# Two fused layers on one core: where the first layer's per-batch mixing stands, before or after the large product

## The reference

```python
att   = softmax(mlp(cond))                          # 32 batches x 8 experts
agg_w = einsum('bk,koi->boi', att, weight)          # a 128x128 matrix of each batch
agg_b = att @ bias_k                                # 128 values of each batch
u     = einsum('boi,bih->boh', agg_w, x) + agg_b[:, :, None]
W_eff = W + sum_e coeffs*scales * Bf_e @ A_e        # 2048x2048, one for all batches
x1    = x + einsum('bsd,od->bso', u, W_eff) + bias
```

## Time and profile before

| | |
|---|---|
| median of 3 runs | 2640.07 us (2638.24 to 2641.44) |
| profiled execution, its own time | 2640.44 us |
| its span, first to last instruction | 2638.5 us |
| PE busy | 2570.8 us, 97% of the span |
| DVE busy | 1837.5 us, 70% |
| ACT busy | 1001.5 us, 38% |
| POOL busy | 955.3 us, 36% |
| DMA | 541.04 MB, mean 205 GB/s |

### The profile page before, as it was taken

The page is one execution under the profiler, slowest core; times in us unless marked ns, Lnnn a source line. Parts: engine busy times, 40 slices in busy tenths (PEclk is TensorE's granted clock), DMA queues, the critical chain, the costliest instruction groups (busy, mean ns, idle before and its releaser), DMA issues. The chain is left out here.

```text
span 2638.5 us, 39106 instructions
## 1 busy us (share of the span) xinstructions
PE 2570.8 (97%) x12090; PEld 2111.6 (80%) x12090; DVE 1837.5 (70%) x2671; ACT 1001.5 (38%) x1631; POOL 955.3 (36%) x826
## 2 busy tenths in 40 slices
PE   7899999999999999999999999999999999999997
PEld 6678888888888888888888778888888888888775
DVE  6555555865555855567444668888888888888776
ACT  3211211322122322233222455555555555555563
POOL 2265654556553554332232312222222222222231
PEclk9999999999999999999999999999999999999998
DMA  8845554755544776576455664576767676767687
GB/s 306 310 168 184 195 174 152 266 170 200 190 156 169 244 226 215 172 239 208 156 167 182 196 178 130 158 219 205 230 206 222 210 223 203 231 212 223 192 272 246
DMA packets 417283, 541.04 MB, mean 205 GB/s; under 512 B 36248, under 2 KB 270064, under 8 KB 417072
## 3 DMA queue, kind: packets, MB, share of 16 engines
q1 hardware_dynamic: 315584, 307.40, 38.9%
q10 hardware_dynamic: 77376, 154.27, 15.6%
q0 software_dynamic: 24112, 76.80, 9.3%
HBM read 309.72 MB, written 228.61 MB: 204 GB/s over the span
## 5 line engine op out<-in xcount | busy, mean ns | idle before, releaser
L427 PE MATMUL ps_c<-w_hi,ring_hi 128*128 128x512 f32 x1792 | 714.1, 398 | 9.6 <-DVE ring_lo L910 5.2
L427 PE MATMUL ps_c<-w_hi,ring_lo 128*128 128x512 f32 x1792 | 708.6, 395 | 0.0
L427 PE MATMUL ps_c<-w_lo,ring_hi 128*128 128x512 f32 x1792 | 708.3, 395 | 0.0
L574 ACT ACTIVATE ring_hi<-raw_n 128x512 fp32r<-128x512 f32 x384 | 241.2, 631 | 901.6 <-DVE raw_n L871 247.3
L1290 POOL DMA_INDIRECT y_d<-y_s,idx x128 | 147.2, 1150 | 736.3 <-ACT y_s L1458 688.0
L427 PEld LDWEIGHTS ps_c<-w_hi,ring_hi 128*128 128x128 f32 x1792 | 338.7, 189 | 87.1 <-DVE ring_lo L910 10.2
L1425 ACT ACTIVATE kern<-ps_up 128x512 f32<-128x512 f32 x512 | 306.2, 598 | 260.3 <-PE ps_up L1308 235.4
L427 PEld LDWEIGHTS ps_c<-w_hi,ring_lo 128*128 128x128 f32 x1792 | 338.4, 189 | 79.2
L427 PEld LDWEIGHTS ps_c<-w_lo,ring_hi 128*128 128x128 f32 x1792 | 338.8, 189 | 76.4
L1542 DVE TENSOR_TENSOR g_lo<-kern,g_hi 128x512 fp32r<-128x512 f32 x512 | 354.7, 693 | 41.0 <-ACT g_hi L1429 20.6
L931 DVE TENSOR_TENSOR r_early<-ps_c,r_early 128x512 f32<-128x512 f32 x256 | 176.8, 691 | 284.3 <-PE ps_c L427 284.3
(11 more groups left out here) (199 smaller groups left out, 3843.5 us busy)
## 6 DMA issues: line engine op xcount, KB each, us to landing
u_d<-raw_n ACTq DMA_DIRECT2D x64, 512.0 KB, 3.3
x_d<-r_early ACTq DMA_DIRECT2D x128, 256.0 KB, 3.4
x_d<-x_s ACTq DMA_DIRECT2D x128, 256.0 KB, 2.6
raw_n<-u_d SPq DMA_DIRECT2D x64, 512.0 KB, 3.7
u_s<-x_d SPq DMA_DIRECT2D x496, 64.0 KB, 2.7
z_d<-x_s SPq DMA_DIRECT2D x120, 256.0 KB
rear<-y_d SPq DMA_DIRECT2D x112, 256.0 KB
rear<-x_d SPq DMA_DIRECT2D x112, 256.0 KB
```

Of the source, the lines that this page charges most:

```text
L427: mm = nc.tensor.matmul(bank, a[:, dc, :], w[k][:, dc, :], start=(first and dc == 0 and n == 0), stop=(dc == 3 and n == 2), skip_group_che ...
L574: nc.scalar.activation(ring_hi[g % RING][:].rearrange("p a n -> p (a n)"), ring_raw[p][k], ACT.Copy).then_inc(hi_ready, 1)
```

## The change

W_eff is applied to x itself, and each batch's mixed matrix afterwards, to the finished pieces.
- SP loads x turned (`x_t`, a further input laid out on the host) straight into `raw`; `make_u`, `take_u`, the store of u and its DRAM array are gone.
- In sweeps 1 and 2 (quads 0 to 15) a piece is only copied out of PSUM and stored (half sums, in `x1_d`). Beside that x + bias is made by POOL in pieces of their own (`res`, a ring of 4; `add_bias`) and stored to a DRAM array `xb_d`.
- In sweeps 3 and 4 (from quad `FINAL` = 16) each of the 8 finished pieces of a quad is split (`split_v` on ACT and DVE), multiplied by its batch's matrix (`mix_v` on PE: 3 matmuls of 512 columns, in slots 6, 7, 12, 13 of the quad and 0 to 3 of the next), and added to x + bias + agg_b times row sum (`take_mixed` on DVE; `add_bias_of_mix` on ACT and `add_e` on POOL make and add the last term). The matrices of a quad are split too (`split_agg`).
- The row sums of W_eff are gathered by POOL and DVE in `sums`, and added over the partitions by two float32 matmuls in slot 5 of quads 16 and 24 (`sum_rows`).
- The ring of split operands has 4 buffers in place of 6, and the operands are made 3 items ahead in place of 4. `EARLY` is 16, so 16 chunks are split in the second layer's steps. The table of rooms is another.
- In the opening the mixed matrices are made in slots 2 and 7 of quad 0, and PE's first products wait for the weights one at a time.

```diff
@@ -38,14 +38,19 @@
 
 
 QUADS = 32
-EARLY = 24
+FINAL = QUADS // 2
+EARLY = 16
 ITEMS = 14
-RING = 6
+RING = 4
 LAST = QUADS * ITEMS
+TRAIL = 8
 HALVES = ((0, 0), (1, 1), (0, 1), (1, 0))
 TILES = 32
 R11, R12, R21, R22 = range(4)
 T_B11, T_B21, T_T2, T_T1, T_T3, T_T4, T_B22 = range(7)
+PIECES = ((R11, 0), (R11, 1), (R22, 0), (R22, 1), (R21, 0), (R21, 1), (R12, 0), (R12, 1))
+MIX_SLOT = (6, 7, 12, 13, 14, 15, 16, 17)
+BIAS_SLOT = (5, 6, 8, 9, 10, 11, 13, 14)
...
         def freed_chunks(q, t):
 
-            n = 2 * (ITEMS * (q - QUADS + 1) + t - 2)
+            n = 2 * (ITEMS * (q - QUADS + 1) + t - 6)
             return range(n, n + 2) if 0 <= n < EARLY else ()
...
-            def load_x(q, j):
-                b = batch(q, j)
-                wait(sp, u_mm, turn(q - 1, j) + 1 if q else 0)
-                if q:
-                    sp.wait_ge(r_set, residuals(q - 1, j // 2, (R12, R21)[j % 2]))
-                sp.dma_start(x_s[j], x[b, :, half_cols(q)]).then_inc(x_or_u_in[j], 16)
...
+            def load_raw(q, j):
+
+                if q == 0:
+                    room_free(sp, (8, 4, 9, 5)[j])
+                else:
+                    sp.wait_ge(lo_ready, ITEMS * (q - 1) + (11 if j % 2 else 13) + j // 2)
+                sp.dma_start(raw[j], x_t[HALVES[sweep(q)][1], batch(q, j), :, :]).then_inc(raw_in[j], 16)
...
+            def load_res(n):
+
+                m = n % 4
+                if n < 4:
+                    room_free(sp, (7, 7, 3, 3)[m])
+                    if m >= 2:
+                        sp.wait_ge(aggw_mm, 8)
+                wait(sp, sh.res_out[m], 16 * (n // 4))
+                sp.dma_start(res[m], piece(x.rearrange("b c (s q) -> b c s q", s=S) if n < 8 * FINAL else xb_d, n)).then_inc(res_in[m], 16)
...
-                if t == 25:
-                    room_free(sp, 6)
-                    load_x(0, 0)
-                    room_free(sp, 7)
-                    load_x(0, 2)
-                if t == 28:
-                    sp.wait_ge(aggb_out, 16)
-                    sp.wait_ge(aggw_out, 16 * 8)
-                    load_agg(0, 0)
-                    load_agg(0, 2)
-                if t == 30:
-                    load_bias(0)
-            for j in (1, 3):
-                room_free(sp, (2, 3)[j // 2])
-                load_x(0, j)
-                load_agg(0, j)
-
...
+                if t in (22, 24, 26, 28):
+                    load_raw(0, {22: 0, 24: 2, 26: 1, 28: 3}[t])
+            room_free(sp, 3)
+            sp.dma_start(experts, cond_w).then_inc(experts_in, 16)
+            room_free(sp, 2)
+            load_bias(0)
...
-            for p in range(2):
-                sp.wait_ge(sh.r_out[p][R11], 16 * QUADS)
-                sp.wait_ge(sh.r_out[p][R22], 16 * QUADS)
+            for m in range(4):
+                sp.wait_ge(sh.res_out[m], 16 * 2 * QUADS)
...
-            def make_u(q, j):
-                n = turn(q, j)
-                pe.wait_ge(x_or_u_in[j], 16 * (q + 1))
-                pe.wait_ge(agg_in[j], 32 * (q + 1))
-                wait(pe, u_ready, n - 1)
-                for dc in range(8):
-                    mm = nc.tensor.matmul(ps_v[:, n % 2, dc * P:(dc + 1) * P], x_s[j][:, dc * P:(dc + 1) * P],
-                                          agg[:, j, :], start=True, stop=True)
-                mm.then_inc(u_mm, 1)
...
+            def mix_v(n):
+
+                i = n - 8 * FINAL
+                blk, p = PIECES[n % 8]
+                j = 2 * p + blk // 2
+                pe.wait_ge(vlo_ready, i + 1)
+                wait(pe, mixed, i - 3)
+                if n % 8 == 0:
+                    pe.wait_ge(agglo_ready, n // 8 - FINAL + 1)
+                if n % 64 == 0:
+                    pe.wait_ge(rs_ready, n // 64 - 1)
+                if n == 8 * 26 + 3:
+                    pe.wait_ge(ctx_read, 1)
+                for a, v in ((agg_hi, v_hi), (agg_hi, v_lo), (agg_lo, v_hi)):
+                    mm = nc.tensor.matmul(ps_w[n % 4], a[:, j, :], v[n % 2][:], start=(a is agg_hi and v is v_hi),
+                                          stop=(a is agg_lo))
+                mm.then_inc(mix_mm, 1)
...
+            def sum_rows(half):
+
+                pe.wait_ge(sums_ready, sums_count(23 if half else 15))
+                pe.wait_ge(aggw_ready, 8)
+                wait(pe, mixed, 64 * half)
+                for n in range(2):
+                    mm = nc.tensor.matmul(ps_w[n], ones[:].to_broadcast([P, P]), sums[half][:, n * 512:(n + 1) * 512],
+                                          start=True, stop=True)
+                mm.then_inc(rs_mm, 1)
...
+            def split_v(n):
+                i = n - 8 * FINAL
+                blk, p = PIECES[n % 8]
+                v_ready(act, n)
+                wait(act, mix_mm, i - 1)
+                nc.scalar.activation(v_hi[n % 2][:], r_s[p][blk], ACT.Copy).then_inc(vhi_ready, 1)
...
+            def add_bias_of_mix(n):
+
+                b, half, sub = place_of(n)
+                act.wait_ge(rs_ready, half + 1)
+                act.wait_ge(res_set, n - 1)
...
+                if n == 8 * 24:
+                    act.wait_ge(mix_out, 16 * 24)
+                nc.scalar.activation(e_room(n), rs_s[:, sub * 512:(sub + 1) * 512], ACT.Identity,
+                                     scale=aggb_s[:, b:b + 1]).then_inc(e_ready, 1)
...
+            def store_res(n):
+                if n < 8 * FINAL:
+                    act.wait_ge(res_set, n + 1)
                 else:
...
+                    act.wait_ge(mixed, n - 8 * FINAL + 1)
+                act.dma_start(piece(xb_d if n < 8 * FINAL else x1_d, n), res[n % 4]).then_inc(sh.res_out[n % 4], 16)
...
-                if ITEMS * q + t + 4 < LAST:
-                    split(ITEMS * q + t + 4)
+                ahead = product_from(q, t, 3)
+                if ahead and ahead != (0, 0):
+                    split(*ahead)
...
+            def add_bias(n):
+                sub = place_of(n)[2]
+                pool.wait_ge(res_in[n % 4], 16 * (n // 4 + 1))
+                pool.wait_ge(bias_in, 16 * (sweep(n // 8) + 1))
+                nc.gpsimd.tensor_tensor(res[n % 4], res[n % 4], bias_s[:, sub * 512:(sub + 1) * 512], ALU.add).then_inc(res_set, 1)
...
-            def take_u(q, j):
-                n = turn(q, j)
-                dve.wait_ge(u_mm, n + 1)
-                dve.wait_ge(agg_in[j], 32 * (q + 1))
-                if q == 0:
-                    room_free(dve, (8, 4, 9, 5)[j])
-                else:
-                    dve.wait_ge(lo_ready, ITEMS * (q - 1) + (11 if j % 2 else 13) + j // 2)
-                    dve.wait_ge(u_out[j], 16 * q)
-                nc.vector.tensor_tensor(raw[j].rearrange("p (c o) -> p c o", o=P),
-                                        ps_v[:, n % 2, :].rearrange("p (c o) -> p c o", o=P),
-                                        bc[:, j, :].unsqueeze(1).to_broadcast([P, 8, P]), ALU.add).then_inc(u_ready, 1)
...
+            def split_v(n):
+                i = n - 8 * FINAL
+                blk, p = PIECES[n % 8]
+                dve.wait_ge(vhi_ready, i + 1)
+                wait(dve, mix_mm, i - 1)
+                nc.vector.tensor_tensor(v_lo[n % 2][:], r_s[p][blk], fp32(v_hi[n % 2][:]), ALU.subtract).then_inc(vlo_ready, 1)
+
+            def take_mixed(n):
+                i = n - 8 * FINAL
+                dve.wait_ge(mix_mm, i + 1)
+                dve.wait_ge(res_set, n + 1)
+                nc.vector.tensor_tensor(res[n % 4], ps_w[n % 4], res[n % 4], ALU.add).then_inc(mixed, 1)
```

More of the change, by code:

```diff
@@ L789, in slot @@
[L789 to L794 removed]
+                    if t in (10, 11):
+                        sum1(q + 1, t - 10)
+                    if t in (12, 13):
+                        sum3(q + 1, t - 12)
+                    if t == 13:
+                        sum2(q + 1, 0)
@@ L795, in slot @@
                         load_early(n)
-                if q == QUADS - 1 and t == 2:
-                    for n in range(4, EARLY):
-                        load_early(n)
-            quads(slot, -7)
+            quads(slot, -4)
         @block.vector
```

590 lines of the change are left out of this document (310 added, 280 removed).

## The result

The changed kernel takes 2761.9 us (2759.96 to 2764.51), against 2640.7 for the kernel before in the same comparison: a ratio of 1.0461, 95% interval 1.0443 to 1.0479. It is 4.6% slower; 2644 was forecast, with a range of 2619 to 2664. The profiled execution has a span of 2758.1 us, 119.6 more than before.

What follows compares the result with a forecast made beforehand. PE, busy for 97% of the span, was taken as the bound. Its work summed to -33.9 us; waits at weight changes and quad 26, seam and second layer made it +3.8: 2644 us, 0.15% more, range 2619 to 2664.

Steps and rivals of the forecast that it cites:

- opening: Tile loads before the first product: SP's stall goes, room waits give back some 2.2 us; -8.5 us, bounds -11 and -3.
- quad 0: First quad: four u's and most of two PE waits go, 42.4 us for 59.9, -17.5.
- quads 1 to 14, first weight change: Without u's 39.07 us a quad, -100.8; PE waiting for DVE's low parts at the first weight change, +3.
- quads 15 to 31, without the last five pieces: Piece matmuls (+89.3 for all 128), row sums +3.6, second and third weight changes +3 and +15, quad 26 +2; +109.4 together.
- seam, with these pieces: Between the layers: a longer chain from last product to barrier, +12.2 us, ends 6 and 16, beside five pieces' matmuls, 3.5.
- second layer: Its start: eight more weight chunks are four more steps, half a microsecond or so each; +2.5 us, ends 0 and 6.
- Rivals 1 and 2: First: stalls are light, 2624 us, chance 0.32. Second: opening gains all, seam costs only 6 for 12.2, 2635, chance 0.06.
- Rival 4: Early quads: transfers land late, each of 8 quads waits 1 us; 2652 us, chance 0.07.
- Rival 3: Late quads: DVE's order binds, one late link is a PE wait, 1 us a quad in 16; 2660 us, chance 0.14.
- Rival 5: Late quads: DVE and POOL instructions run one after the other, 4.1 us a quad; 2698 us, chance 0.05.
- Weight changes: PE waits for late DVE: +3 us at each of the first two, +15 at the third (13 waiting, 2 lower clock).
- In quad 26: Slot 5: context matmuls wait for the last piece of quad 25, three DVE instructions ahead; +2 us.

Runs made afterwards that it cites:

- the relaxed order: Changed kernel with every weight-piece step placed behind the one it waits for, and ACT's store of x + bias one slot later: 2699.6 us, ratio 1.0236.

## Why the prediction was wrong

By its own terms, in span (quad starts of both traces):

| term | forecast | measured |
|---|---|---|
| opening | -8.5 | -9.3 (first product at 116.34 for 125.61) |
| quad 0 | -17.5 | -18.2 |
| quads 1 to 14, first weight change | -97.8 | -30.7 (617.1 for 647.8) |
| quads 15 to 31, without the last five pieces | +109.4 | +153.2 (817.4 for 664.2) |
| seam, with these pieces | +15.7 | +18.3 |
| second layer | +2.5 | +6.3 |

**The step that failed** is "Quads 1 to 14 without u's: 14 x 39.07 = 547.0", with its sentence that they keep their cover. I priced what PE does in such a quad and took from the quads with u's that nothing else is late there. The change had moved the weight pieces to earlier slots, put two DVE additions between load and mixing, and queued additions that ACT waits for behind them on POOL. All three stand in the whole diff (the part printed above shows the last alone), and no term of the sum speaks of a weight piece. That is 66 us in sweeps 1 and 2 and 25 in sweep 3. The cause of the 66 is shown: with the relaxed order and all the work these quads take 39.1 us each on the mean. Of the 25 it is shown that they go with the third sweep's weight pieces, 44.5 us a quad without them, but not by which link.

**Rivals 1 and 2** had less loss than the forecast; the changes of weights, the seam and the second layer's start, on which they rest, all cost more than it has. **Rival 4** (late transfers in the early quads, 0.07) was the nearest, by its place; its mechanism is refuted, and its 8 us were an eighth of the loss. **Rival 3** (a late link is a wait for PE, quads 16 on) had the shape of what happened in quads 17 to 20, at 6 us a quad in place of 1, but quads 25 and 27 to 30, which it counted too, take 44.5 to 44.8. **Rival 5**, the port lock: DVE and POOL do hold each other up (below), but it had 16 quads at 4.1 us above their matmuls, and the steady ones take 44.5, nothing above them.

**Weight changes.** The first cost 5.6 us for 3 (quad 8, 44.6), the second 7.9 for 3: quad 16 takes 51.5 us, of which 39.0 + 2.8 + 1.8 are matmuls, and PE waits in it three times for low parts of items (2.56, 2.01 and 0.61 us). Both go with the pass for x + bias, 0.6 us each without it; whether by contention or by its waits and transfers was not taken apart. The third: quads 23 and 24 take 114.6, of which 39.0 + 5.6 and 39.0 + 5.6 + 1.8 are matmuls, so 23.6 are lost for 15. In front of the row sums PE waited 7.40 us, and then ran at half clock (granted 0.50 from 1244.34 to 1248.09):

```profile
1244.34 3.75 PE L497 MATMUL ps_v<-kern,ones 128*128 128x512 f32 x4 [7.40 <-DVE x_n L1031]
```

The wait was foretold at this place, and "10 us and more" was too much: part of the lateness is met before it, at a take (3.0) and a result piece (4.1). The mechanism stands, and the waits were nearly sized: PE is idle for 15.8 us in the two quads, where 13 were forecast. The clock was not: PE is busy for 46.69 and 52.14 us with 91.0 us of matmuls, so 7.8 us are matmuls at the lower clock, where the forecast has 2. In quad 26 5.3 us for 2.

**What was right.** The pieces' matmuls cost the pitch (44.5 for 39.0 a quad is 5.5 for 24, and 5.6 was forecast), the row sums' pair 1.9 at full clock (the eight records of L497 are 5.6 us, 3.75 of them behind the wait).

The opening and quad 0 came within 1 us, the opening in part by luck. Between the last addition of a tile and the first product, before and after:

```profile
120.43 1.23 DVE L829 TENSOR_TENSOR raw_n<-ps_c,raw_n 128x1024 f32<-128x1024 f32 x1 [1.51 <-PE ps_c L393]
...
116.21 1.22 DVE L923 TENSOR_TENSOR x_s<-ps_c,x_s 128x1024 f32<-128x1024 f32 x1
116.34 0.50 PE L469 MATMUL ps_c<-w_hi,ring_hi 128*128 128x512 f32 x1 [0.38 <-DVE ring_lo L960]
```

The tiles end 4.2 us earlier, where the forecast had 8.5 for the stall less the rooms. Another 4.8 are the wait in front of the first product, 0.38 us for 5.21. That wait stands before 125.61 and so belongs to the opening; the forecast had put it into quad 0. Quad 0 before has the wait of 4.14 alone in its window, and six u's, not four (two of its own and the four of quad 1; its other two stand in the opening, at 109.48 and 115.71). The 42.4 that were forecast for it were added up from what stays, 41.8 measured, and so do not suffer. Two smaller slips: the timeline's u is 1.92 less 0.23, 1.69 us and not 1.80, and rows 7 do show float32 matmuls of 512 columns, though on 32 rows.

The second layer's term was short, 6.3 us for 2.5, and the kernel before with 16 early chunks shows it as the chunks' price (7.7). The seam's chain was read rightly, and it cost 2.6 us more than its term; its last loads (issued at 1602.67, behind a store issued at 1598.93) are the link:

```profile
1592.55 0.40 PE L469 MATMUL ps_c<-w_hi,ring_lo 128*128 128x512 f32 x1
...
1602.67 1.38 SPq L354 DMA_DIRECT2D x_n<-xb_d  x2
...
1606.01 1.26 POOL L820 TENSOR_TENSOR x_n<-x_n,mix 128x512 f32<-128x512 f32 x1 [3.98 <-DMA x_n<-xb_d]
...
1609.03 0.69 DVE L1031 TENSOR_TENSOR x_n<-ps_v,x_n 128x512 f32<-128x512 f32 x1 [0.96 <-POOL x_n L820]
...
1614.88 0.76 PE L1439 MATMUL ps_c<-xp_hi,cw_hi 128*128 128x512 f32 x1 [10.03 <-DVE xp_lo L1594]
```

**Open.** Why a weight piece in the third sweep costs 2.7 to 3.1 us wherever it is laid is not settled: POOL's additions and the loads behind them come later, but which link PE meets was not taken apart. Nor is it settled by what the pass for x + bias costs the first two changes of weights: no run with all of its work brought quad 16 below 49.1 us, for 43.6 of matmuls.

## What to carry to other kernels

Before a quad is costed by its matmuls, follow each shared buffer once round its cycle (load, each engine that touches it, store) and set that beside the slots that it is given; then ask what is queued behind each of its waits on every engine. The same early slots cost nothing in one kernel and were most of a loss of 66 us in another, where two row sums had come into the cycle and the additions behind it were awaited by the engine that feeds all the others. The parts of a kernel that a change removes (here u) may be the slack that hid such a cycle; no run here tests that. And a forecast of a wait on PE needs a term for the clock behind it: here it was 7.8 us beside 15.8 of waiting, and 21 beside 44.
